# Filling stacked attention rows by direct copies, and an expert stage with plain f32 products, norms inside its tile loop and scattered output rows

## What is computed

```python
x = LN(x + gate(x))                  # SSIM-like token weights and channel weights on a projected value
a = LN(MHA16(q=x+pe, k=ctx+pe, v=ctx+pe) + (x+pe)) # cross attention, 16 heads of 16 features
a = LN(relu(a @ W1.T + b1) @ W2.T + b2 + a)
x4 = LN(x + a)
x5 = LN(x4 + MHA16(x4, x4, x4))      # self attention with biases
gp = softmax(x5 @ w_group + b_group) # 4 groups
ep = softmax(x5 @ w_expert + b_expert) # 2 experts in each
e  = best expert of the best group;  gate = its two probabilities multiplied
moe = gate * (relu(x5 @ w1[e] + b1[e]) @ w2[e] + b2[e])   # 8 experts, hidden 512
out = LN(LN(x5 + moe) + x4)
```

## Time and profile before

| what | us |
| --- | --- |
| median of 3 runs | 1010.25 (1004.70 to 1012.99) |
| the profiled execution | 1008.04 |
| its span, first to last instruction | 1006.1 |
| gate stage, from the span's start to | 86.5 |
| attention stage, to | 802.0 |
| ahead of the tile loop, to | 851.2 |
| tile loop, to | 947.1 |
| gathers, norms and output, to | 1006.1 |

### The profile page before, as it was taken

How to read it: one execution, slowest core, us unless ns; L and a number is a source line. 1 busy time by engine, 2 the same in 40 slices (tenths; PEclk the granted TensorE clock), 3 DMA queues, 4 the chain that set the end, 5 groups by cost and what they waited for, 6 DMA issues and landing times. The chain is left out here.

```text
span 1006.1 us, 12601 instructions
## 1 busy us (share of the span) xinstructions
PE 681.6 (68%) x4120; PEld 452.7 (45%) x4121; DVE 516.7 (51%) x1231; ACT 260.9 (26%) x382; POOL 167.2 (17%) x172
## 2 busy tenths in 40 slices
PE   5844487676977868688885967977668551999500
PEld 4723254443644445355553544544434320787400
DVE  3874235353654635356364454544535283555276
ACT  2101040313324222142240413413132260222102
POOL 3003310102201102020120202101010035000063
PEclk9976687978989879797797978969796655999855
DMA  5555331505224051433213334223140092222323
GB/s 214 159 177 203 90 80 28 136 13 147 65 53 117 25 122 33 115 96 69 69 60 89 85 83 97 66 53 80 37 116 12 19 311 83 62 64 68 110 69 99
DMA packets 58989, 92.51 MB, mean 92 GB/s; under 512 B 7665, under 2 KB 46005, under 8 KB 55481
## 3 DMA queue, kind: packets, MB, share of 16 engines
q1 hardware_dynamic: 52650, 79.39, 29.2%
q0 software_dynamic: 1680, 7.21, 2.1%
q10 hardware_dynamic: 4608, 5.24, 1.5%
HBM read 58.01 MB, written 33.29 MB: 91 GB/s over the span
## 5 line engine op out<-in xcount | busy, mean ns | idle before, releaser
L1351 DVE TENSOR_REDUCE a_nmax<-wide 128x4 f32<-128x1024 f32 x128 | 153.0, 1218 | 150.7 <-PE wide L981 150.5
L981 PE MATMUL wide<-a_K,a_Q 48*128 48x256 f32 x512 | 74.0, 394 | 103.2 <-DMA a_Q<-pack_d 98.5
L1193 ACT ACTIVATE a_E<-wide 128x1024 f32<-128x1024 f32 x128 | 125.0, 1015 | 46.1 <-PE wide L981 46.1
L863 POOL TENSOR_TENSOR a_rstd<-a_var,nhalf 128x2 f32<-128x2 f32 x40 | 27.9, 698 | 580.5 <-DVE a_var L1316 580.5
L1172 ACT ACTIVATE a_th<-bank 128x512 f32<-128x512 f32 x48 | 28.7, 598 | 367.9 <-PE bank L928 367.9
L981 PEld LDWEIGHTS wide<-a_K,a_Q 48*128 48x128 f32 x512 | 49.7, 248 | 139.1 <-issue 128.0
L134 PE MATMUL bank<-a_th,dw 128*128 128x256 f32 x320 | 94.2, 445 | 6.3 <-ACT a_th L1172 6.2
L134 PE MATMUL bank<-dw,a_th 128*128 128x256 f32 x320 | 98.2, 436 | 0.0
L134 PEld LDWEIGHTS bank<-dw,a_th 128*128 128x128 f32 x320 | 66.5, 219 | 34.0 <-issue 20.6
L134 PEld LDWEIGHTS bank<-a_th,dw 128*128 128x128 f32 x320 | 66.2, 217 | 26.0 <-ACT a_th L1172 14.7
L981 PE MATMUL wide<-a_Q,a_K 50*128 50x256 f32 x512 | 63.5, 332 | 20.8 <-ACT a_E L1193 20.0
(11 more groups left out here) (262 smaller groups left out, 1103.2 us busy)
## 6 DMA issues: line engine op xcount, KB each, us to landing
pack_d<-a_stage SPq DMA_DIRECT2D x64, 256.0 KB, 2.4
a_K<-pack_d SPq DMA_DIRECT2D x32, 256.0 KB, 4.5
a_Q<-pack_d SPq DMA_DIRECT2D x32, 256.0 KB, 4.2
w<-in_w_dram SPq DMA_DIRECT2D x1, 4096.0 KB
a_K<-pack_d SPq DMA_DIRECT2D x32, 128.0 KB, 3.5
a_Q<-pack_d SPq DMA_DIRECT2D x32, 128.0 KB, 4.8
x_d<-a_x SPq DMA_DIRECT2D x16, 256.0 KB, 4.7
m_w<-in_w_dram SPq DMA_DIRECT2D x1, 4096.0 KB, 21.1
```

The costliest lines, as they stand in the source:

```text
L863: pool.tensor_tensor(rstd[l][:, :], var[l][:, :], nhalf[:, 0:T], ALU.pow).then_inc(rs_ok[l].s, 1)
L981: last = pe.matmul(pW[r % 2][:, c * 512 + e * S:c * 512 + (e + 1) * S], left[l][part_, s, tok(t)], right[l][part_, s, :], start=True, stop ...
L1193: act.activation(Ex[g % 2][:, kt, :, :], pW[r % 2][:, :].rearrange("p (h s) -> p h s", h=4), ACT.Exp, scale=HD ** -0.5).then_inc(ex.s, 1)
L1351: dve.tensor_reduce(nmax[l][:, t, :].rearrange("p (h c q e) -> p h q c e", h=HALVES, c=C, q=2)[:, jj // 2, jj % 2, :, :], pW[r % 2][:, :]. ...
```

## The change

1. *Gate stage.* A row of `xs_d` gets 514 columns: `x5`, `x4`, the gate and the number of the token. The buffer is filled from one blank row that is broadcast; in it the token number is 2048, one beyond the last.
2. *Stacks.* `pack_d` goes. `stack` copies the high part from `stage` into its two blocks of partitions of `K` or `Q` as soon as it is there (four DMAs of 128 KB), and the low part into the third block (two DMAs). The wait for the end of the attention before (`cx_tr`), which stood between writes and reads, now stands ahead of all six. Every position table is rewritten.
3. *Expert stage.* Weights are not split; all expert products are plain f32. The biases are split into two parts of 8 rows each and enter each product as a matmul with a 16-row selection of the tile's expert. `x5` and `x4` are loaded next to each other, with gate and token number, and scattered together. The loop over tiles is written out; it loads six tiles ahead. In it VectorE makes both norms of each tile, POOL the powers, ScalarE the last scaling, and POOL scatters the finished rows to the output by their token numbers, where the rows of padding fall out of bounds and are left out. `ys_d`, the gathers and the pass after the loop go.

The diff, cut to its core (the tables of ScalarE and POOL are rewritten in the same way; `done(engine, s, c)` waits for tile c on semaphore s; the second norm is written like the first):

```diff
--- before
+++ after
 TILES = NT + E - 1
+ROW = 2 * D + 2
...
-    pack_d = scratch("pack_d", (2, 2, C, 2, P, S))
     x4_d = scratch("x4_d", (B, P, T * D))
     x5_d = scratch("x5_d", (B, P, T * D))
-    xs_d = scratch("xs_d", (TILES * P, D))
-    ys_d = scratch("ys_d", (TILES * P, D))
+    xs_d = scratch("xs_d", (TILES * P, ROW))
...
-            pool.memset(zeros[:, :], 0.0).then_inc(zero_ok, 1)
-            pool.wait_ge(zero_ok, 1)
-            pool.dma_start(xs_d.rearrange("(p n) d -> p (n d)", p=P), zeros[:, :]).then_inc(zero_out, 16)
+            pool.memset(blank[:, 0:2 * D + 1], 0.0).then_inc(zero_ok, 1)
+            pool.memset(blank[:, 2 * D + 1:ROW].bitcast(I32), B * S).then_inc(zero_ok, 1)
+            pool.wait_ge(zero_ok, 2)
+            pool.dma_start(xs_d.rearrange("(p n) d -> p n d", p=P),
+                           blank[:, :].unsqueeze(1).to_broadcast([P, TILES, ROW])).then_inc(zero_out, 16)
...
 AT_PE = {
-    "own": {0: 5.5, 1: 10, 2: 12.35, 3: 12.35, 4: 16.95},
+    "own": {0: 5.75, 1: 9.25, 2: 12.1, 3: 13.35, 4: 16.2},
     "tail": {0: 0, 2: 0},
-    "middle": {0: 1.5, 2: 3.5, 3: 4.25, 6: 5.5, 8: 6, 9: 6.25, 11: 8.5, 12: 9.5, 16: 13.25, 18: 14.45, 19: 14.5, 21: 14.95, 22: 14.95, 24: 15.95, 25: 16.45},
-    "last": {0: 2.5, 2: 3.25, 3: 4, 6: 11.5, 8: 12.75},
-    "first": {0: 6, 2: 6, 3: 6.25, 4: 6.5, 5: 7.5, 6: 8, 7: 9, 10: 12.75, 12: 14, 13: 14.75},
+    "middle": {0: 0, 2: 0, 3: 0, 6: 1, 8: 3, 9: 4.25, 11: 6.25, 12: 7, 16: 14.95, 18: 16.95, 19: 16.95, 21: 16.95, 22: 16.95, 24: 16.95, 25: 16.95},
+    "last": {0: 0, 2: 0.25, 3: 1.25, 6: 7.75, 8: 15},
+    "first": {0: 2.5, 2: 3.75, 3: 4.25, 4: 5.5, 5: 6.5, 6: 8, 7: 10.75, 10: 15, 12: 16.45, 13: 16.7},
 }
...
 AT_DVE = {
-    "own": {0: 5.75, 1: 10.75, 2: 11.95, 3: 12, 4: 16.45},
-    "tail": {1: 0, 3: 0.5},
-    "middle": {4: 4.5, 5: 4.75, 13: 9.75, 14: 11.25, 15: 11.5, 20: 12.2, 23: 12.2, 26: 13.5},
-    "last": {4: 4.25, 5: 8.5, 9: 14.25},
-    "first": {3: 6, 8: 8.75, 9: 11.25, 14: 16.2},
+    "own": {0: 5.75, 1: 8.75, 2: 12.95, 3: 14.45, 4: 15.2},
+    "tail": {1: 0, 3: 0},
+    "middle": {4: 0, 5: 0, 13: 8.95, 14: 9.75, 15: 10.7, 20: 16.2, 23: 16.7, 26: 16.95},
+    "last": {4: 1.75, 5: 2.25, 9: 12.7},
+    "first": {3: 4.25, 8: 8.75, 9: 10, 14: 16.95},
 }
...
 AT_SP = {
-    "own": {0: 3.5, 1: 8.5},
+    "own": {0: 0.5, 1: 12.75},
     "tail": {},
-    "middle": {4: 11, 20: 11.45, 23: 12.25, 26: 16.45},
-    "last": {5: 8.5},
-    "first": {5: 4.25, 14: 8.95},
+    "middle": {4: 0, 20: 15.2, 23: 16.7, 26: 16.95},
+    "last": {5: 8},
+    "first": {5: 8.45, 14: 15.2},
...
-            def stack(i, l, a, x_, lo0, lo, w, r, tile, parts):
+            def stack(i, l, a, x_, hi, lo0, lo, r, tile, hi_rows, lo_row):
+                sp.wait_ge(cx_tr[l].s, cx_tr[l].at(i, a - 1))
+                sp.wait_ge(hi[l].s, hi[l].at(i, a))
+                for c in range(C):
+                    for row in hi_rows:
+                        sp.dma_start(tile[l][64 * c + row:64 * c + row + HD, :, :].bitcast(F32),
+                                     stage[l][:, x_, c, 0, :].bitcast(F32)).then_inc(r[c][l].s, 16)
                 for c in range(C):
                     if c == 0:
                         sp.wait_ge(lo0[l].s, lo0[l].at(i, a))
                     else:
                         sp.wait_ge(lo[l].s, lo[l].at(i, a))
-                    sp.wait_ge(r[c][l].s, r[c][l].at(i, a - 1))
-                    sp.dma_start(pack_d[l, x_, c].rearrange("m p t -> p m t"), stage[l][:, x_, c, :, :].bitcast(F32)
-                                 ).then_inc(w[c][l].s, 16)
-                sp.wait_ge(cx_tr[l].s, cx_tr[l].at(i, a - 1))
-                for c in range(C):
-                    sp.wait_ge(w[c][l].s, w[c][l].at(i, a))
-                    for row, m, lo_, hi_ in parts:
-                        sp.dma_start(tile[l][64 * c + row:64 * c + row + m, :, :].bitcast(F32),
-                                     pack_d[l, x_, c, lo_:hi_].rearrange("m (d s) t -> (m d) s t", s=HC)
-                                     ).then_inc(r[c][l].s, 16)
+                    sp.dma_start(tile[l][64 * c + lo_row:64 * c + lo_row + HD, :, :].bitcast(F32),
+                                 stage[l][:, x_, c, 1, :].bitcast(F32)).then_inc(r[c][l].s, 16)
             def stack_q(i, l, a):
-                stack(i, l, a, 0, q_lo0, q_lo, q_w, q_r, Q, ((0, 2 * HD, 0, 2), (2 * HD, HD, 0, 1)))
+                stack(i, l, a, 0, q_hi, q_lo0, q_lo, q_r, Q, (0, 2 * HD), HD)
             def stack_k(i, l, a):
-                if i == 0:
+                if i == 0 and a == 0:
                     sp.wait_ge(ones_ok, 3 * (l + 1))
-                stack(i, l, a, 1, k_lo0, k_lo, k_w, k_r, K, ((0, HD, 0, 1), (HD, 2 * HD, 0, 2)))
+                stack(i, l, a, 1, k_hi, k_lo0, k_lo, k_r, K, (0, HD), 2 * HD)
...
-            def heads_hi(i, l, x_, bank, mm, w, a, done):
+            def heads_hi(i, l, x_, bank, mm, r, a, done):
                 act.wait_ge(mm[l].s, mm[l].at(i, a))
                 for c in range(C):
-                    act.wait_ge(w[c][l].s, w[c][l].at(i, a - 1))
+                    act.wait_ge(r[c][l].s, r[c][l].at(i, a - 1))
...
+            sp.dma_start(bias[:, 0:F], I["b1"]).then_inc(b_in, 16)
+            sp.dma_start(bias[:, F:], I["b2"]).then_inc(b_in, 16)
             sp.dma_start(cst[:, :], I["cst"].partition_broadcast(P)).then_inc(cst_in, 16)
-            sp.dma_start(x5[:, :, :].rearrange("p (b t) d -> p b (t d)", t=T), x5_d.rearrange("b p n -> p b n")
-                         ).then_inc(x5_in, 16)
+            for b in range(B):
+                sp.dma_start(xr[:, b * T:(b + 1) * T, 0:D], x5_d[b].rearrange("p (t d) -> p t d", t=T)).then_inc(x5_in, 16)
+            for b in range(B):
+                sp.dma_start(xr[:, b * T:(b + 1) * T, D:2 * D], x4_d[b].rearrange("p (t d) -> p t d", t=T)
+                             ).then_inc(x4_in, 16)
             sp.dma_start(w2[:, :, :, :], I["w2"].rearrange("e (c p) f -> p e c f", p=P)).then_inc(w_in, 16)
-            sp.dma_start(b2[:, :, :], I["b2"].partition_broadcast(P)).then_inc(b2_in, 16)
+            sp.wait_ge(b_lo, 1)
+            sp.dma_start(bs[E:2 * E, :].bitcast(F32), bl[:, :].bitcast(F32)).then_inc(bl_in, 16)
             sp.wait_ge(xs_w, 16 * NT)
...
+            for c in range(TILES):
+                done(sp, u_ok, c - XB)
+                sp.dma_start(xs[c % XB][:, :], xs_d[c * P:(c + 1) * P, :]).then_inc(xs_in[c % XB], 16)
+                if c == XB - 1:
+                    sp.dma_start(ids[:, :, :], xs_d.rearrange("(t p) d -> p t d", p=P)[:, :, GATE:TOKEN + 1].bitcast(I32)
+                                 ).then_inc(ids_in, 16)
...
+            pool.wait_ge(b_hi, 1)
+            pool.tensor_tensor(bl[:, :], bias[:, :], bs[0:E, :].bitcast(F32), SU).then_inc(b_lo, 1)
+            pool.wait_ge(x5_in, 16 * B)
+            pool.wait_ge(x4_in, 16 * B)
+            pool.wait_ge(id_ok, 2)
             pool.wait_ge(slot_ok, 1)
             for n in range(NT):
                 pool.indirect_dma_start(out=xs_d, out_offset=bass.IndirectOffsetOnAxis(ap=slot[:, n:n + 1], axis=0),
-                                        in_=x5[:, n, :], in_offset=None).then_inc(xs_w, 16)
...
+            flat_out = out.rearrange("b s d -> (b s) d")
+            for c in range(TILES + 4):
+                if there(c):
+                    done(pool, var1_ok, c)
+                    pool.tensor_tensor(rstd1[c % 2][:, :], var1[c % 2][:, :], nhalf[:, 0:1], ALU.pow).then_inc(rs1_ok, 1)
+                if there(c - 1):
+                    done(pool, var2_ok, c - 1)
+                    done(pool, o_ok, c - 1 - UB)
+                    pool.tensor_tensor(rstd2[(c - 1) % UB][:, :], var2[(c - 1) % UB][:, :], nhalf[:, 0:1], ALU.pow
+                                       ).then_inc(rs2_ok, 1)
+                if there(c - 3):
+                    if c == 3:
+                        pool.wait_ge(ids_in, 16)
+                    done(pool, o_ok, c - 3)
+                    pool.indirect_dma_start(out=flat_out, out_offset=bass.IndirectOffsetOnAxis(
+                                                ap=ids[:, c - 3, 1:2], axis=0),
+                                            in_=o[(c - 3) % 2][:, :], in_offset=None, bounds_check=B * S - 1,
+                                            oob_is_err=False).then_inc(out_w[(c - 3) % 2], 16)
...
+                if there(c + 1):
                     l = (c + 1) % 2
+                    e = expert(pe, c + 1)
+                    done(pe, hb_ok, c - 1)
+                    pe.matmul(pH[l][:, :], sel[:, c + 1, :], bs[:, 0:F], start=True, stop=False)
+                    done(pe, xT_ok, c + 1)
+                    plain(pe, pH[l][:, :], [xT[l][:, k, :] for k in range(C)],
+                          [w1[:, bass.ds(e, 1), k, :].rearrange("p o f -> p (o f)") for k in range(C)], False
+                          ).then_inc(h_mm, 1)
+                if there(c - 1):
                     l = (c - 1) % 2
```

(55 more changed lines are left out.)

446 lines of the change are left out of this document (137 added, 309 removed).

## The result

The changed kernel takes 1035.53 us (median of 4 runs, 1031.47 to 1037.79), the kernel before 1007.49 beside it: a ratio of 1.0267, with a 95% interval of 1.0205 to 1.0329. It is slower by 2.7%. 879 us had been forecast, with a range of 845 to 935.

What follows compares the result with a forecast made beforehand. It took the attention stage to dominate, with TensorE waiting for stacked query rows and at a lowered clock. 1006.1 - 70 - 18 - 3 - 1 + 1 - 6 + 15 - 47 = 877 us span, plus 1.9: 879, range 845 to 935.

Steps and rivals of the forecast that it cites:

- Position tables, SP's row: Stack copies in SP's queue: six issues either way, some 2.6 us, 5.2 for a pair of stacks.
- the slower rival: Stack copies: at 2.1 us or more each, the whole attention gain of 131 us goes, 1010 to 1080; chance 0.03.
- Cost of a copy: Stacks: 0.65 us per 128 KB copy into 16 partitions, 7.8 us a pair; bounds 0.43 and 1.3.
- the first rival: Stack copies slow: 1.3 us each, 15.6 a pair against 12 of cover, plus 65, so 944; chance 0.12.
- the prediction's own signs of being wrong: Stacked-row wait above 4 us; long periods over 42 with a wait elsewhere; or POOL or VectorE busiest in the tile loop.
- Cover by moved work: Attention boundaries: moved products cover the copies for 10 to 13 us; long periods minus 8.8 each, short ones minus 2.6.
- The row for the clock: Attention stage: the changed kernel's profile should show a granted clock of 0.88 or more.
- Gate stage and first attention: Larger fill of the sorted buffer plus 1 us, bounds nothing and plus 10; first attention loses one landing, minus 3.
- Ahead of the tile loop: Stretch before the loop: without weight splits all scatters take 1.26 us with gaps; minus 6, bounds minus 9 and 0.
- Output scatters beside VectorE: Tile loop: VectorE's two-port operations block descriptor writing, so each output scatter costs 2.2 us, not 1.26.
- Tile loop: Expert tiles: TensorE paces at 4.5 us a tile, bounds 3.75 and 4.9; 110.5 us for 95.9, plus 15.
- Tail: After the loop: the 59.0 us of gathers and norms go, 11.5 remain after the last product; minus 47.

Runs made afterwards that it cites:

- copies_old_order: Kernel before with direct copies into the stacked rows; old position tables, fill and expert stage kept: 1001.18 us, 0.9898 of the kernel before.
- best: Changed kernel with the position tables of the kernel before; direct copies, new fill and new expert stage kept: 983.37 us, 0.9711 of the kernel before.
- maxima_first: Changed kernel with one table number altered, putting the second half of the maxima rows ahead of the key copies in SP's queue: 979.48 us, 0.9677.
- attn_only: Kernel before with direct copies and new position tables together; old fill and old expert stage: 1051.12 us, 1.0389 of the kernel before.
- moe_only: Kernel before with the new expert stage and new fill; stacks through DRAM and old order: 996.55 us, 0.9858 of the kernel before.
- relay_copies: maxima_first with the second block of high rows copied from the first stacked block once landed, not from the staging tile: 971.89 us, 0.9633.
- thin_copies: maxima_first with each stack copy after the first pair moving 16 KB in place of 128 KB: 923.62 us, 0.9128 of the kernel before.

## Why the prediction was wrong, step by step

- **Position tables, SP's row (failed, some 60 us).** I costed SP's issues as "six either way" and looked at the copies' own landing. What is queued behind the copies, and who waits for that, was never asked, so the sum has no term for it: it is the maxima rows, and the second scores of every short period wait for them. Key copies and second "own" step stand in the queue in the old order (4.25 and 8.5 before, 8.45 and 12.75 after). But the new tables have the second maxima ready 5.1 us after the first and not 7.5, while the issues between them grew: one copy takes 0.6 us to issue, not the 0.43 of a read, and the store of `x5` now stands there too. No rival had this mechanism; the slower rival had put the loss on the copies.
- **Cost of a copy (mis-sized).** 0.65 us was taken; 1.1 were measured, within the bounds of 0.43 and 1.3, and near the first rival's price. That rival's place was right, and its size roughly: with the maxima first, some 52 us hang on the copies where 65 had been worked out. Two of the prediction's own signs of being wrong came with it: the long periods end in waits of 2.7 to 5.9 us for the stacked rows, where none over 3 had been named, and stay at 45.7 us.
- **Cover by moved work (failed in the long periods).** "Minus 8.8" and "minus 2.6" took the moved products as cover and their old place as gained. (The long periods before average 46.8 us, 45.1 to 48.0; the prediction's 47.1 left out the last.) With copies at nearly no cost the short periods do come to 33.1 us on average, 4.3 under before, but the long ones to 42.8, 4.0 under. What had run between the rounds of scores now stands alone between two attentions: from the last second scores to the next first ones there were 13.1 us before, 20.3 after, and 16.6 without the copies. What the long periods win in their second half (15.2 to 10.9 us) they give back there. The runs of the parts say the same: the copies alone gain some 10 us (copies_old_order), and the new order, with the maxima first, adds some 12 by the profiled spans of best and maxima_first, which the ratios don't resolve; the two together had been put at 92. The row for the clock named under "what would show it", 0.88 or more, came out at 0.78.
- **Gate stage and first attention (mis-sized, 6.6 us).** Minus 2 was forecast, plus 4.6 came. The fill's 5.9 MB land after 27.2 us, where 2.9 MB took 10.1, and the first attention still waits 9.83 us for its rows. The fill is what costs: with the old fill the first scores start at 117.25 us (attn_only), with the new one and all else old at 124.35 (moe_only), with both old at 118.55.
- **Ahead of the tile loop (right).** The scatters all take 0.97 us, as the earlier trace rows has it for those without a weight split beside them; 44.7 us for the stretch, 4.5 less, where 6 had been forecast.
- **Output scatters beside VectorE (the row decided).** The 2.2 us each that the prediction drew from the earlier trace rows by the Trainium skill (SBUF — State Buffer, the box on DVE blocking DMA) did not come: 1.02 us each beside VectorE's norms, within 6% of the 0.97 of the scatters ahead of the loop, most of which run beside an idle VectorE. The box speaks of two-port operations. No run shows that the weight splits or the norms are such operations, so the agreement that the prediction saw isn't shown. A scatter and its gap beside the splits, 1.9 and 0.3 us, come to what one split takes (8.89 us for four); the norms' operations take 0.5 us or less.
- **Tile loop (mis-sized).** 4.5 us were taken and 5.22 measured, above even the upper bound of 4.9. The bound counted the eight products and the transposes and left out the two bias products; these are the 1.12 us. The products and transposes alone take 4.10, under the estimate. The first tiles also run at a granted clock of 0.65, after TensorE had stood still for 32 us: 16.5 us pass from the first transpose to the first finished product. In all, plus 31 from the first transpose (893.66) to the last finished product (1020.7) in the place of plus 15.
- **Tail (right).** From the last finished product to the end 14.0 us, minus 45, where minus 47 had been forecast.

The terms add up: 131 us of the 158 between forecast and measured span lie in the attention stage, 6.6 ahead of it, 16 in the tile loop, 4 in the rest. Of the 131, the maxima rows in SP's queue account for some 60 and the time of the copies for some 52 by the runs; the other 19 or so lie in the long periods by the reading above, and no run isolates them.

Of the kernels that compute everything, relay_copies and maxima_first are the fastest, 3.7% and 3.2% under the kernel before; they are not told apart, nor is best from either.

## What to carry to other kernels

When steps of several engines are reordered, write out for each queue what stands in front of what, and when each becomes ready: here small and large DMAs stood in the queue as before, but four small DMAs became ready while six large ones were still being issued ahead of them, and that turned a gain of 3% into a loss of 3%. When a part of the old tables is put back to find the cause, look in the trace for waits that only the mixture has. A step moved in front of a wait is a gain only if the place that it leaves gets shorter; look at what bounds that place. And count every small product of a loop body, with the gap at its weights: two of 0.5 and 0.4 us made a fifth of a tile.

## What was not expected of the hardware

- Copies between on-chip rows into 16 partitions kept all DMA engines occupied at 102 to 130 GB/s, where the same rows were read from DRAM at 182 to 201 GB/s (two thirds of those bytes into 32 partitions); with pieces of 8 KB, read from 16 partitions, they were no faster.
- How full the DMA engines are did not change the time of an issue on SP: a copy's issue took 0.6 us in the median both where the engines were occupied and where they had room. A few took 1.1 to 1.9 us (4 of 192 in the changed kernel, one of them in the 3.79 us above), in thin_copies too, where the engines were nearly idle.
- A wait of 4 us in the middle of an attention cost 8 us, with the granted clock of the period going from 0.88 to 0.78.
